# Attention with position bias on one core: query buffers, the order of turns, scaled copies and last keys, and a value copy per head

## The reference

```
q, k, v = heads of x @ Wq, x @ Wkv                     # 16 heads, 2048 x 64 each
sim  = q k^T / 8
P    = min(reverse cumulative sum of sigmoid(sim), 63)
sim += interpolation of (q @ pos_emb) at position P    # per query and key
attn = softmax(sim);  out = attn @ v;  out @ Wout + b_out
```

## Time and profile before

| | us |
|---|---|
| median of 3 runs (lowest, highest) | 2278.76 (2276.46, 2284.88) |
| profiled execution, its own time | 2286.39 |
| its span | 2284.3 |
| TensorE busy in the span | 2191.0 (96%) |
| ScalarE busy | 1752.7 (77%) |
| VectorE busy | 1633.2 (71%) |
| GpSimd busy | 389.5 (17%) |
| 100 to 1780 us of the span: TensorE, ScalarE, VectorE busy | 1641.4, 1437.6, 1412.8 of 1680 |

### The profile page before, as it was taken

How to read it: one execution, slowest core, us unless ns; L and a number is a source line. 1 busy time by engine, 2 the same in 40 slices (tenths; PEclk the granted TensorE clock), 3 DMA queues, 4 the chain that set the end, 5 groups by cost and what they waited for, 6 DMA issues and landing times. The chain is left out here.

```text
span 2284.3 us, 53247 instructions
## 1 busy us (share of the span) xinstructions
PE 2191.0 (96%) x14577; PEld 1487.9 (65%) x14577; DVE 1633.2 (71%) x4269; ACT 1752.7 (77%) x3723; POOL 389.5 (17%) x673
## 2 busy tenths in 40 slices
PE   7999999999999999999999999999998979999997
PEld 5666666666666666666666666666665557777775
DVE  5888888888888888888888888888888811323231
ACT  5888888888888888888888888888888843454543
POOL 1111111111111111111111111111111101212121
PEclk9999999999999999999999999999999989999997
DMA  2010101010101010101010101010001021010100
GB/s 65 24 32 25 30 24 30 24 30 26 30 25 31 23 30 24 30 24 30 24 30 24 30 24 30 24 31 25 24 15 48 13 67 35 30 39 30 39 30 7
DMA packets 107087, 67.04 MB, mean 29 GB/s; under 512 B 27821, under 2 KB 104814, under 8 KB 106990
## 3 DMA queue, kind: packets, MB, share of 16 engines
q1 hardware_dynamic: 106990, 65.56, 10.7%
HBM read 14.33 MB, written 2.10 MB: 7 GB/s over the span
## 5 line engine op out<-in xcount | busy, mean ns | idle before, releaser
L843 DVE TENSOR_REDUCE mx<-Sc 128x1 f32<-128x1024 f32 (+1 forms) x512 | 564.6, 1128 | 225.9 <-PE Sc L632 225.9
L482 ACT ACTIVATE probsT<-rings 128x512 f32<-128x512 f32 x1024 | 542.6, 601 | 180.9 <-PE rings L640 180.8
L506 ACT ACTIVATE probs<-Sc,nbias 128x1024 f32<-128x1024 f32 x512 | 568.8, 1125 | 28.1 <-DVE nbias L853 28.0
L640 PEld LDWEIGHTS rings<-ident,probs 128*128 128x128 f32 x4096 | 447.3, 143 | 203.2 <-issue 122.4
L640 PE MATMUL rings<-ident,probs 128*128 128x128 f32 x4096 | 530.8, 278 | 2.2 <-ACT probs L506 2.2
L632 PE MATMUL Sc<-qk,q_now 64*128 64x512 f32 x2048 | 506.6, 607 | 26.5 <-ACT probs L506 12.5
L654 PE MATMUL out<-probsT,V 128*64 128x256 f32 x4096 | 498.3, 384 | 19.0 <-issue 9.8
L654 PEld LDWEIGHTS out<-probsT,V 128*64 128x64 f32 x4096 | 311.8, 136 | 140.6 <-issue 65.9
L806 DVE COPY_PREDICATED z<-mask,z 128x224 f32<-128x224 int16 (+5 forms) x768 | 394.6, 514 | 11.3
L374 POOL TENSOR_TENSOR prod<-cut,z 128x350 f32<-128x350 f32 x128 | 120.5, 941 | 1460.0 <-DVE z L818 1460.0
L632 PEld LDWEIGHTS Sc<-qk,q_now 64*128 64x128 f32 x2048 | 182.6, 186 | 186.3 <-issue 172.1
(11 more groups left out here) (128 smaller groups left out, 2292.0 us busy)
## 6 DMA issues: line engine op xcount, KB each, us to landing
q_now<-qk SPq DMA_DIRECT2D x256, 64.0 KB, 2.0
xv<-xT SPq DMA_DIRECT2D x113, 128.0 KB, 2.2
q_far<-qk SPq DMA_DIRECT2D x256, 32.0 KB, 1.8
at<-attn SPq DMA_DIRECT2D x16, 512.0 KB, 3.2
probs<-in_x_dram SPq DMA_DIRECT2D x4, 512.0 KB, 5.6
wqk<-in_L_attn_Wq_dram SPq DMA_DIRECT2D x32, 64.0 KB, 2.1
xin<-in_x_dram SPq DMA_DIRECT2D x16, 128.0 KB, 2.8
out_dram<-res SPq DMA_DIRECT2D x16, 128.0 KB, 1.7
```

What stands on the lines that cost most here:

```text
L482: nc.scalar.activation(probsT[:, u, 4 * s:4 * s + 4, :], ring[SLOT_BANK[k]][:, :].rearrange("p (t q) -> p t q", q=P), ACT.Copy).then_inc(s ...
L506: nc.scalar.activation(probs[:, u, cols], Sc[:, cols], ACT.Exp, bias=nbias[:, u:u + 1], accum_out=sums[:, u, half:half + 1]).then_inc(exp_ ...
L640: last = nc.tensor.transpose(ring[SLOT_BANK[k]][:, j * P:(j + 1) * P], probs[:, u, (4 * s + j) * P:(4 * s + j + 1) * P], ident[:, :])
L843: nc.vector.tensor_reduce(mx[:, u, half:half + 1], Sc[:, cols], AX.X, ALU.max).then_inc(dve_unit, 1)
```

## The change

q_now gets two buffers, used by odd and even bodies in turn; SyncE loads the queries of body g+1 at the start of its body g, once the logits of body g-1 are done, ahead of q_far. On TensorE the turns stand directly behind the two late sets and not behind set 1 of tile 1; on ScalarE the scaled copies move likewise. In the last body of each head ScalarE copies the projected queries and keys between the two exponentials of tile 1 and not after them; for this its loop over bodies becomes a loop over heads with an inner loop of six bodies and two written out. The values of the current head are copied by one transfer per head from V to V_now, from which TensorE reads; it is issued once the outputs of the head ahead are done, and TensorE waits for it at the first outputs of a body.

```diff
+        V_now = sb("V_now", [P, NT, C])
...
-        q_now = sb("q_now", [P, 2 * P])
+        q_now = sb("q_now", [P, 2, 2 * P])
...
             def load_now(g, odd):
                 h, t = g // PAIRS, g % PAIRS
-                sp.dma_start(q_now[0:C, :], queries(h, odd, t)).then_inc(now_in, 16)
-                sp.dma_start(q_now[C:P, :], queries(h, odd, t)).then_inc(now_in, 16)
+                for r in range(2):
+                    sp.dma_start(q_now[r * C:(r + 1) * C, int(odd), :], queries(h, odd, t)).then_inc(now_in, 16)
...
+            def load_values(g):
+
+                sp.dma_start(V_now[:, :, :], V[:, (g // PAIRS) % 4, :, :]).then_inc(v_in, 16)
...
-            def body(g, odd, late=False, first=False, tile=True, far=True, near=False):
+            def body(g, odd, late=False, first=False, tile=True, far=True, now=True, head=False, near=False):
                 base = slots_before(g, late)
+                if now:
+
+                    if not first:
+                        wait_apart(sp, bank_full, g * 4, waited)
+                    wait_apart(sp, now_in, g * 32 + 32, waited)
+                    load_now(g + 1, not odd)
                 if far:
...
-                wait_apart(sp, bank_full, g * 4 + 4, waited)
-                load_now(g + 1, not odd)
+                if head:
+
+                    wait_apart(sp, out_full, g, waited)
+                    load_values(g)
...
@@ ScalarE, body @@
                 if not first:
                     transposed(0, base, at.late, (2, 3))
-                    transposed(1, base, at.last, (0, 1))
                     if not second:
                         scale(g - 2, 0)
                         scale(g - 2, 1)
-                    transposed(1, base, at.last, (2, 3))
+                    transposed(1, base, at.last)
...
                 exp_half(g, 1, 0)
+                if proj and keys_first:
+                    project(g + PAIRS, not odd, base, at.qk, SLOT_BANK[at.qk], alone=not val)
                 exp_half(g, 1, 1)
                 if not first:
                     empty_halves(g - 1)
-                if proj:
+                if proj and not keys_first:
                     project(g + PAIRS, not odd, base, at.qk, SLOT_BANK[at.qk], alone=not val)
...
+            with act.Fori(1, LASTV // PAIRS) as h:
+                with act.Fori(0, PAIRS - 2, 2) as t:
+                    body(h * PAIRS + t, False)
+                    body(h * PAIRS + t + 1, True)
+                body(h * PAIRS + PAIRS - 2, False)
+                body(h * PAIRS + PAIRS - 1, True, keys_first=True)
...
@@ TensorE @@
             def outputs(g, base, slots, tiles, empty=True):
...
                         wait_apart(pe, scaled, g * 2, waited)
+                    wait_apart(pe, v_in, g // PAIRS * 16 + 16, waited)
...
-                    last = nc.tensor.matmul(out[half:half + C, 0:2 * P], V[:, keys % 4, token_tile(t), :],
+                    last = nc.tensor.matmul(out[half:half + C, 0:2 * P], V_now[:, token_tile(t), :],
...
                     transposes(0, base, at.late, 3, late_before)
+                    if not second:
+                        turns_of(g - 2)
                     transposes(1, base, at.last, 0, late_before)
                     transposes(1, base, at.last, 1)
-                    if not second:
-                        turns_of(g - 2)
                     transposes(1, base, at.last, 2)
```

More of the change, by code:

```diff
@@ L322, in _ @@
             with sp.Fori(1, LASTV // PAIRS - 1) as h:
[L323 removed]
+                body(h * PAIRS, False, head=True)
                 body(h * PAIRS + 1, True, near=True)
@@ L329, in _ @@
                 weights(h + 2)
-            body(LASTV - PAIRS, False)
+            body(LASTV - PAIRS, False, head=True)
             body(LASTV - PAIRS + 1, True, near=True)
@@ L335, in _ @@
             weights(H - 1, values=False)
-            body(LASTV, False, tile=False)
+            body(LASTV, False, tile=False, head=True)
             body(LASTV + 1, True, tile=False, near=True)
@@ L342, in _ @@
             load_early(sp, A, A["ctx_in"])
-            body(LASTP, False, late=True, tile=False)
+            body(LASTP, False, late=True, tile=False, head=True)
             body(LASTP + 1, True, late=True, tile=False)
@@ L507, in exp_half, with body @@
                                      accum_out=sums[:, u, half:half + 1]).then_inc(exp_done, 1)
-            def body(g, odd, late=False, first=False, second=False, proj=True, val=True, far=True, near=True):
+            def body(g, odd, late=False, first=False, second=False, proj=True, val=True, far=True, near=True,
+                     keys_first=False):
                 base = slots_before(g, late)
@@ L624, in _, with logits @@
                     window(1, 0)
-            def logits(par, u, half):
+            def logits(par, odd, u, half):
                 cols = slice(half * BANK, (half + 1) * BANK)
@@ L631, in logits @@
                     bank = half * 2 + r
-                    last = nc.tensor.matmul(Sc[:, bank * BANK:(bank + 1) * BANK], q_now[rows, u * P:(u + 1) * P],
+                    last = nc.tensor.matmul(Sc[:, bank * BANK:(bank + 1) * BANK], q_now[rows, int(odd), u * P:(u + 1) * P],
                                             qk[rows, par, r, cols], start=True, stop=True)
@@ L642, in transposes, with outputs @@
                 last.then_inc(slot_full, 1)
-            def outputs(g, base, slots, tiles, keys, empty=True):
+            def outputs(g, base, slots, tiles, empty=True):
                 if tiles[0] == 0:
@@ L684, in body @@
                     transposes(0, base, at.late, 3, late_before)
+                    if not second:
+                        turns_of(g - 2)
                     transposes(1, base, at.last, 0, late_before)
                     transposes(1, base, at.last, 1)
-                    if not second:
-                        turns_of(g - 2)
                     transposes(1, base, at.last, 2)
                     transposes(1, base, at.last, 3)
-                    outputs(g - 1, base, at.last, range(EARLY_TILES), keys, empty=not second)
+                    outputs(g - 1, base, at.last, range(EARLY_TILES), empty=not second)
                 if far:
@@ L703, in body @@
                 if not first:
-                    outputs(g - 1, base, at.last, range(EARLY_TILES, NT), keys)
+                    outputs(g - 1, base, at.last, range(EARLY_TILES, NT))
                 if proj:
```

45 lines of the change are left out of this document (25 added, 20 removed).

## The result

The changed kernel takes 2291.48 us (median of 5 runs, 2290.33 to 2294.52) against 2279.95 us for the kernel before, run beside it (median of 5 runs, 2276.46 to 2284.88): a ratio of 1.0053, 95% interval 1.004 to 1.0066. The forecast was 2282 us, no change. The result lies inside the outer range of 2260 to 2297 us, but 1.5 us above the forecast's own range (2272 to 2290). The measured loss is small and real: 11.5 us, 0.5%, which is just at the line between "same" and "slower" that the prediction drew; the interval has both sides of it.

The account below looks back on a forecast made before the run. TensorE's chain through the early outputs was taken to bound the kernel. From a 2278.8 us median, +8.8 (order) -4.3 (buffers) +1.2 (q_far) -1.5 (keys) gave 2283, rounded down to 2282 us; own range 2272 to 2290, outer 2260 to 2297.

Parts of the forecast that it names:

- What bounds the kernel: TensorE's chain per body: moving the early outputs against P, the start of a body's transposes, moves the body, 126 times.
- Turns and scaled copies: Reordering on TensorE and ScalarE: early outputs at P (start of transposes) +3.51 instead of +3.44, +8.8 us in all.
- mechanism of the bank: Set 3 of the transposes reuses set 0's bank, so it waits for ScalarE's copy of set 0, behind the scaled copies.
- The 0.07 us: Predicted delay of the early outputs in each body from exchanging one wait for another; times 126 gives +8.8 us.
- second rival: First scaled copy of each body waits for the turns; slower from P (start of transposes) +1.95; 2302 us, chance 0.18.
- first rival: Bank does not hold the transposes, TensorE runs at its own pace: -0.16 us a body, 2254 us; chance 0.18, shared.
- Two buffers: Query loads a body earlier remove q_now waits and three others: -8.6 us, half counted; +1.2 us once for q_far.
- "nothing" for q_far at a head start: Two q_now issues ahead of q_far take about 1.2 us, leaving 0.9 us spare, so no cost at head starts.
- the prediction's own signs of being wrong: Outputs at P (start of transposes) +3.3, scaled copy after P+1.95, V_now or head-start q_far waits, period not following early outputs.
- Last keys: At 15 head starts, key copy between exponentials brings second-half logits 0.11 us earlier: about -1.5 us, bounds -9 to +7.
- The value copy: One 512 KB transfer a head, landing 2.9 us early, and one long-satisfied wait at the first output: cost nothing.
- ScalarE's longer program: Rival: longer ScalarE loop code brought in at each head, 15 times perhaps 1 us: 2297 us; chance 0.07 with late transfers.

## Why the prediction came out as it did

**What bounds the kernel.** Right. With the kernel before, three kernels that move the start of the early outputs show it (P+3.21, 3.32 and 3.52, against 3.44), and the body follows: 13.75, 13.86 and 14.08, against 13.98.

**Turns and scaled copies.** The mechanism of the bank was right: the wait for the scaled copies is exchanged for the bank of set 3, the copy of set 0 ends 0.64 us ahead of the outputs as in body 1, and the outputs come at P+3.52, predicted 3.51. The sum of +8.8 us was too small: the piece alone measures +13 us (12 by the ratio). The 0.07 us was read from one body; over the bodies it is 0.07 to 0.12, from 13.95 to 13.99 before to 14.06 and 14.10.

That the scaled copies start where it was said (P+1.87, predicted 1.86) is luck, because the reason was wrong. The 0.67 us behind the copy ahead was read as mostly the end of that copy. They wait for the turns, and then for their address, and they did so before the change too: the earlier trace rows have the turns' end at 1012.59 and the first scaled copy 0.42 later, and the lag is 0.38 to 0.42 in the loop's bodies of both kernels. In the new order it happens to give the same start. That is the second rival's mechanism, 0.05 us below where that rival was said to begin to hurt; by the prediction's own sum it begins at P+1.92 and not 1.95, since 0.125 us a body already gives 2290 us. The first rival, that the bank does not hold, is out for this order.

**Two buffers.** No wait for q_now is left, as predicted. How much of the -8.6 us a median run has is not shown: alone the edit is -2 us, with 3.7 us more of q_far waits. With the scaled copies out of the way and q_far first, the second buffer gives 8 us. The failed step is "nothing" for q_far at a head start. It took 1.2 us for the two issues ahead; measured are 1.72 us from the first q_now issue to the first of q_far, with semaphore and register instructions between them in the queue. That alone still fits into the 2.1 us that were spare in the earlier trace rows. But those were read from one head start with quick weights; where a transfer of weights is slow to issue as well (1.53 us in the queue above), q_far is late. A wait for q_far at head starts was one of the prediction's own signs of being wrong, and it came, 10 times; the others did not.

**Last keys.** Predicted -1.5 us, measured the wrong side: the second logits come 0.27 us later at 14 of 15 head starts, some +4 us. The failed step is the start of the key copy: it was put 0.24 us after the successor of its projection starts, as for transposes; here it is 0.46 (1052.27 to 1052.73), and the exponential behind it pays for it. The logits then came 1.49 after that exponential's start, where 1.35 was used. What the 0.24 left out is again address work, which now stands between the projection and the copy. At that head start the view of line 432 has this register instruction of 0.15 us

```profile
L432 ACTq FUSED_REGOPS  x1: 152/152/152, 1052.5 to 1052.5; - x1
```

ahead of the copy. At the end of the first head, where the same copy of 256 columns is written out with a fixed place, there is no such row:

```profile
143.72 0.61 PE L621 MATMUL rings<-wv,xv 128*128 128x128 f32 x4
143.93 0.47 ACT L432 ACTIVATE qk<-rings,qk_scale 128x256 f32<-128x256 f32 x1
```

The copy starts 0.21 us after the successor, the second logits 1.53 after the first, and nothing is lost. No run changes the address alone here.

**The value copy.** Right in the change (nothing: its periods are those of the moved order alone), but partly by luck: "one more wait, which is long satisfied" is not free by itself.

**ScalarE's longer program.** The rival was priced at +1 us a head; the sign is the other one, -4.7 us (0.9977), with no sign of reloaded code in the periods. It is a term that the sum didn't have, and it brought the change back towards no change. Nor is the loop as long as the rival took it: in the code it has four bodies (two in the inner loop, two written out), and the trace has some 50 records of ScalarE to a body, so an estimate of 200 instructions, less than the two lines of 256 that the prediction set against it.

**The sum.** Measured pieces: +13 (order) -2 (buffers) -5 (loops) +3 (keys) +0 (values) = +9 us, against +11.5 for the whole. The rest is within what the runs of the kernel before differ by; it wasn't pursued. So the forecast came near because its misses offset each other: order, q_far and keys each cost more than it had, and the loops gave back what it didn't have.

## What to carry to other kernels

When a wait is removed by a new order, write down which resource each moved instruction now stands ahead of: here two small copies moved ahead of the one copy whose bank the next engine needed next, and one place further back they cost nothing and gave 26 us. Measure a change of several parts part by part: this one held +13, +3, -2 and -5 us and the possibility of -33. Put a wait that is satisfied early ahead of the one that is satisfied last.

## What the runs showed that was not expected

- A satisfied wait on TensorE costs 0.15 us a body when it stands last (14.13 against 13.98), nothing when first (13.98), and at most 0.04 in a kernel where the waits ahead of it no longer hold anything.
- ScalarE's addresses for two small copies cost 0.20 us between the release and the start (0.38 against 0.18), before the change as after; a body whose indices need less work, written out, took 0.15 us less (13.82 against 13.95, 14.46 against 14.62) as long as those copies held the chain, and nothing less where they did not.
- The copy of a projection of 256 columns started 0.46 us after TensorE's next group where its place was computed, and 0.21 where it was fixed.
